# A gated cross-attention and mixture-of-experts block: three-product scores, a staged GpSimd, and new orders of work

## The reference, cut to what matters

```python
# x: (4, 256, 128)   ctx: (4, 256, 96)   2 heads of 64, 32 experts of 64, top 4
def _L0_xattn_ref(x, latents, mask, ...):
    xn = layernorm(x, ln_x_g, ln_x_b);  ln = layernorm(latents, ln_l_g, ln_l_b)
    q = ln @ Wq.T
    kv = jnp.concatenate([xn @ Wkv.T, ln @ Wlkv.T], axis=1)      # 512 keys
    k, v = (kv[..., :INNER], kv[..., INNER:])
    qn = rmsnorm(q, qn_g) * SCALE;  kn = rmsnorm(k, kn_g)
    attn = jnp.einsum('bhid,bhjd->bhij', qn, kn)                 # masked, softmax
    out = jnp.einsum('bhij,bhjd->bhid', attn, v)
    return out @ Wo.T + bo
def _L0_ffn_ref(x, expert_sel, keys, values):
    gates = jax.nn.sigmoid(jnp.einsum('nd,ed->ne', xt, expert_sel))
    sel_val, sel_idx = jax.lax.top_k(gates, 4)                   # gate_full: the 4 kept
    scores = jax.nn.relu(jnp.einsum('nd,edf->nef', xt, keys)) * gate_full[:, :, None]
    return jnp.einsum('nef,efv->nv', scores, values)
x = x + jnp.tanh(g_xattn[0]) * _L0_xattn_ref(ctx_768, _layernorm(x), mask, ...)
x = x + jnp.tanh(g_ffn[0]) * _L0_ffn_ref(_layernorm(x), expert_sel, keys, values)
```

## Time and profile before

| | |
|---|---|
| median of three runs | 115.79 us |
| the profiled execution's own time | 115.75 us |
| its span on the core | 114.0 us |
| TensorE busy | 105.8 us (93%) |
| VectorE busy | 95.0 us (83%) |
| ScalarE busy | 65.6 us (58%) |
| GpSimd busy | 16.0 us (14%) |
| share of TensorE in the chain that ended last | 74% |

### The profile page before, as it was taken

One profiled execution on the slowest core, in us unless ns is written; L12 is line 12 of the kernel. 1 busy time (PEld: TensorE's weight loads), 2 busy tenths in 40 slices (PEclk: granted clock), 3 DMA queues, 4 the chain that ended last, 5 costly groups with the idle time before them and its releaser, 6 DMA issues.

```text
span 114.0 us, 2086 instructions
## 1 busy us (share of the span) xinstructions
PE 105.8 (93%) x644; PEld 86.1 (76%) x644; DVE 95.0 (83%) x309; ACT 65.6 (58%) x148; POOL 16.0 (14%) x26
## 2 busy tenths in 40 slices
...
GB/s 86 223 179 397 376 10 3 3 6 0 0 0 0 6 0 0 0 3 6 0 12 49 297 270 255 178 255 198 3 12 285 299 244 229 214 126 83 0 30 154
DMA packets 7112, 12.78 MB, mean 112 GB/s; under 512 B 894, under 2 KB 2558, under 8 KB 6847
## 3 DMA queue, kind: packets, MB, share of 16 engines
...
HBM read 12.00 MB, written 0.66 MB: 111 GB/s over the span
## 4 chain that ended last, share of the span: by engine, by line
PE 74%; ACT 12%; DMA 4%; DVE 3%; SPq 3%; issue 1%; DVEq 1%
PE bank L724 13%; PE bank L726 13%; PE bank L725 13%; PE bank L862 10%; PE bank L849 5%; DMA bo<-wb_in 4%; PE bank L916 3%; PE bank L754 3%; PE bank L783 3%; PE bank L794 2%; PE bank L820 2%; PE bank L847 2%; ACT cx L594 1%; ACT kT L657 1%; PE bank L887 1%
## 5 line engine op out<-in xcount | busy, mean ns | idle before, releaser
L701 ACT ACTIVATE hid_hi<-keys 128x512 fp32r<-128x512 f32 x28 | 17.4, 632 | 16.8 <-DVE keys L535 13.1
L535 DVE SCALAR_TENSOR_TENSOR keys<-bank,inT 128x512 f32<-128x512 f32 x32 | 21.2, 686 | 1.1 <-PE bank L726 0.8
L552 DVE TENSOR_TENSOR hid_lo<-keys,hid_hi 128x512 fp32r<-128x512 f32 x28 | 18.4, 686 | 0.1
L862 PE MATMUL bank<-vw,prob 128*128 128x129 f32 x128 | 15.7, 278 | 0.2 <-ACT prob L670 0.2
L862 PEld LDWEIGHTS bank<-vw,prob 128*128 128x128 f32 x128 | 14.8, 191 | 1.0 <-issue 1.0
L724 PE MATMUL bank<-xm_hi,k_lo 128*128 128x512 f32 x32 | 13.7, 427 | 0.0
L726 PE MATMUL bank<-xm_hi,k_hi 128*128 128x512 f32 x32 | 12.5, 391 | 0.0
L725 PE MATMUL bank<-xm_lo,k_hi 128*128 128x512 f32 x32 | 12.5, 390 | 0.0
L445 DVE CUSTOM_DVE_ANT_0 junk<-bank,mask_b 128x512 bf16<-128x512 f32 x16 | 10.4, 689 | 2.0 <-PE bank L820 1.8
L724 PE MATMUL bank<-hid_hi,v_lo 128*128 128x512 f32 x28 | 11.3, 402 | 0.0
L670 ACT ACTIVATE prob<-bank 128x512 f32<-128x512 f32 x16 | 8.7, 594 | 4.0 <-PE bank L849 3.8
...
## 6 DMA issues: line engine op xcount, KB each, us to landing
...
```

What stands on the lines that cost most here:

```text
L535: dve.scalar_tensor_tensor(hid[:, n % 3, :], bank[H_BANK[n % len(H_BANK)]][:, :], 0.0, gated[:, n % SLOTS, :], ALU.max, ALU.mult).then_inc ...
L552: dve.tensor_tensor(hid_lo[:, m % RING, :], hid[:, n % 3, :], hid_hi[:, m % RING, :].bitcast(F32), ALU.subtract).then_inc(hid_lo_ready, 1)
L701: act.activation(hid_hi[:, m % RING, :], hid[:, n % 3, :], ACT.Copy).then_inc(hid_hi_ready, 1)
L862: last = pe.matmul(bank_of(b, OUT + t)[:, WOA * a:WOA * a + WOA], prob[:, b % 2, a, j, P * t:P * t + P], vw[:, b, j, a, :], start=(j == 0) ...
```

## The change

- **Scores.** `qT`, `kT` in f32 and `round_qk` go. ScalarE writes the rounded `qT_hi`, `kT_hi` straight from PSUM; a new stage `turn_qk` on VectorE computes `qT_lo`, `kT_lo` = PSUM times gain minus the rounded part. Each f32 product of `weights` becomes three fp32r products. `row_max` reuses the banks, so it now waits for the low parts too.
- **GpSimd** gets a table, POOL_ORDER. It takes over the Newton steps (four operations there, since its step is written without the fused form), `xn` and `xm`, the split of the selection weights, the `+ 1` of the sigmoid and the scaling of `bo`.
- **Residual.** `turn_res` transposes straight into the accumulator banks, ahead of the `down` sums, with no copy; tanh(g_ffn) moves into the gates. `finish` only copies: ScalarE for the first half, VectorE for the second.
- **Orders.** All tables are new. On ScalarE `constants` comes ahead of the first `stats_in` and no longer holds the scaling of `bo`. The 24 `warm` stages stay, 15 instead of 19 of them ahead of the first transposes.

```diff
-    warm 13, warm 14, warm 15, warm 16, warm 17, warm 18, turn_in 0, warm 19, warm 20, project 0, turn_in 1,
-    fold 0, project 1, vctx 0, vlat 0, turn_in 2, vlat 1, warm 21, warm 22, turn_qk 0, vctx 1, warm 23, vlat 2,
+    warm 13, warm 14, turn_in 0, warm 15, warm 16, warm 17, fold 0, project 0, turn_in 1, vlat 0, warm 18,
+    warm 19, project 1, warm 20, vctx 0, vlat 1, turn_in 2, vctx 1, turn_qk 0, warm 21, vctx 2, turn_qk 1,
...
+POOL_ORDER = """
+    norm_in 0, norm_in 1, mask 0, norm_in 2, scale_bo 0, newton_qk 0, newton_qk 1, split_sel 0, add_bias 0,
+    norm_in 3, newton_qk 2, low_keys 0, newton_qk 3, add_bias 1, low_values 0, low_values 1, low_keys 1,
+    norm_mid 0, low_keys 2, low_keys 3, norm_mid 1, add_one 0, add_one 1, norm_mid 2, low_values 2, add_one 2,
+    norm_mid 3, low_values 3, add_one 3
...
+            def newton(y, v, w):
+
+                then(pool.tensor_tensor(w[:, 1, :], y, y, ALU.mult))
+                then(pool.tensor_tensor(w[:, 2, :], w[:, 1, :], v, ALU.mult))
+                then(pool.tensor_scalar(w[:, 1, :], w[:, 2, :], -0.5, 1.5, ALU.mult, ALU.add))
+                return pool.tensor_tensor(w[:, 3, :], w[:, 1, :], y, ALU.mult)
...
+            def norm_in(b):
+                pool.wait_ge(var_ready, b + 1)
+                pool.tensor_scalar(nm_in[:, b, :], mv_in[:, b, BT:, 0], -1.0, None, ALU.mult)
+                pool.wait_ge(y0_in, b + 1)
+                then(newton(rs_in[:, b, 0, :], var_in[:, b, :], rs_in[:, b, :, :]))
+                pool.tensor_tensor(nb_in[:, b, :], nm_in[:, b, :], rs_in[:, b, 3, BT:], ALU.mult).then_inc(nb_ready, 1)
+                for t in range(BT):
+                    j = BT * b + t
+                    pool.tensor_scalar(xn[:, j, :], x[:, j, :], mv_in[:, b, t, 0:1],
+                                       rs_in[:, b, 3, t:t + 1], ALU.subtract, ALU.mult).then_inc(xn_ready, 1)
...
+            def turn_qk(b):
+
+                dve.wait_ge(qk_hi_ready, 2 * b + 1)
+                dve.scalar_tensor_tensor(qT_lo[:, b, :], bank_of(b, TURN_QK + 1)[:, 0:S], gq[:, :],
+                                         qT_hi[:, b, :].bitcast(F32), ALU.mult, ALU.subtract).then_inc(qk_lo_ready, 1)
+                dve.wait_ge(qk_hi_ready, 2 * b + 2)
+                dve.scalar_tensor_tensor(kT_lo[:, b, :], bank_of(b, TURN_QK)[:, :], vec(V_KG),
+                                         kT_hi[:, b, :].bitcast(F32), ALU.mult, ALU.subtract).then_inc(qk_lo_ready, 1)
...
                 for b in range(HB * h, HB * h + HB):
-                    dve.wait_ge(midT_ready, b + 1)
-                    dve.wait_ge(down_done, EC * (h + 1))
-                    dve.scalar_tensor_tensor(res[:, b, :], bank[ACC_BANK[h]][:, S * (b % HB):S * (b % HB) + S],
-                                             tanh_g[:, 1:2], x_midT[:, b, :], ALU.mult, ALU.add).then_inc(res_ready, 1)
-
+                    dve.tensor_copy(res[:, b, :], acc(b)).then_inc(res_ready, 1)
...
-                act.wait_ge(in_bo, 16)
-                act.activation(bo[:, :], bo[:, :], ACT.Copy, scale=tanh_g[:, 0:1]).then_inc(bo_ready, 1)
...
-                    if i >= 2:
+                    if i < 2:
+                        pe.wait_ge(qk_lo_ready, 2 * b + i + 1)
+                    else:
                         pe.wait_ge(max_taken, n - 1)
...
                     for a in range(HEADS):
-                        last = pe.matmul(o[a], kT[rows[a], b, keys_t], qT[rows[a], b, :], start=False, stop=True)
+                        pe.matmul(o[a], kT_lo[rows[a], b, keys_t], qT_hi[rows[a], b, :], start=False, stop=False)
+                    for a in range(HEADS):
+                        pe.matmul(o[a], kT_hi[rows[a], b, keys_t], qT_lo[rows[a], b, :], start=False, stop=False)
+                    for a in range(HEADS):
+                        last = pe.matmul(o[a], kT_hi[rows[a], b, keys_t], qT_hi[rows[a], b, :], start=False, stop=True)
...
-                    last = pe.transpose(res_bank(b)[:, P * t:P * t + P], x_mid[:, BT * b + t, :], ident[:, :])
-                last.then_inc(midT_done, 1)
+                pe.wait_ge(gateT_ready, HB * (b // HB + 1))
+                for t in range(BT):
+                    pe.matmul(acc(b)[:, P * t:P * t + P], x_mid[:, BT * b + t, :], ident[:, :],
+                              start=(b % HB == 0 and t == 0), stop=False, is_transpose=True)
```

More of the change, by code:

```diff
@@ new lines @@
+    warm 19, project 1, warm 20, vctx 0, vlat 1, turn_in 2, vctx 1, turn_qk 0, warm 21, vctx 2, turn_qk 1,
+    warm 22, row_max 0.0, warm 23, vlat 2, turn_in 3, row_max 0.1, project 2, vlat 3, row_max 1.0, turn_max 0,
+    vctx 3, weights 0.0, row_max 1.1, project 3, turn_qk 2, turn_max 1, weights 0.1, weights 1.0, row_max 2.0,
+    attend 0.0, attend 0.1, turn_qk 3, weights 1.1, row_max 2.1, row_max 3.0, attend 1.0, turn_max 2,
+    row_max 3.1, weights 2.0, attend 1.1, turn_mid 0, weights 2.1, turn_max 3, select 0, weights 3.0, attend 2.0,
@@ L72 @@
 """
 DVE_ORDER = """
-    stats_in 0, stats_in 1, norm_in 0, norm_in 1, scale_wo 0, stats_in 2, sum_qk 0, norm_in 2, sum_qk 1,
-    norm_qk 0, stats_in 3, norm_qk 1, norm_in 3, row_max 0.0, row_max 0.1, row_max 1.0, turn_max 0, sum_qk 2,
-    norm_qk 2, sum_qk 3, row_max 1.1, norm_qk 3, turn_max 1, row_max 2.0, row_max 2.1, row_max 3.0, turn_max 2,
-    out_proj 0, stats_mid 0, row_max 3.1, norm_mid 0, out_proj 1, turn_max 3, stats_mid 1, turn_mid 0,
-    norm_mid 1, select 0, turn_mid 1, select 1, out_proj 2, stats_mid 2, norm_mid 2, out_proj 3, turn_mid 2,
@@ L84 @@
[L84 to L85 removed]
+    stats_in 0, scale_gq 0, stats_in 1, scale_wo 0, stats_in 2, sum_qk 0, stats_in 3, sum_qk 1, norm_qk 0,
+    norm_qk 1, turn_qk 0, row_max 0.0, turn_qk 1, row_max 0.1, sum_qk 2, turn_max 0, row_max 1.0, norm_qk 2,
+    row_max 1.1, turn_max 1, turn_qk 2, sum_qk 3, row_max 2.0, norm_qk 3, out_proj 0, turn_qk 3, row_max 2.1,
+    row_max 3.0, turn_max 2, stats_mid 0, row_max 3.1, out_proj 1, turn_mid 0, turn_max 3, stats_mid 1, select 0,
@@ L86 @@
+    up 1.8, up 1.9, split 1.7, split 1.8, split 1.9, up 1.10, up 1.11, up 1.12, split 1.10, split 1.11, up 1.13,
+    split 1.12, up 1.14, up 1.15, split 1.13, split 1.14, split 1.15, finish 1
 """
 ACT_ORDER = """
-    stats_in 0, constants 0, stats_in 1, norm_in 0, turn_in 0, norm_in 1, project 0, turn_in 1, stats_in 2,
-    fold 0, project 1, norm_in 2, sum_qk 0, vctx 0, vlat 0, turn_in 2, sum_qk 1, vlat 1, turn_qk 0, stats_in 3,
-    vctx 1, round_qk 0, turn_qk 1, norm_in 3, round_qk 1, turn_in 3, vlat 2, vctx 2, split_keys 0, project 2,
@@ L91 @@
-    vlat 3, vctx 3, sum_qk 2, weights 0.0, project 3, weights 0.1, sum_qk 3, turn_qk 2, round_qk 2, split_keys 1,
-    split_values 0, turn_qk 3, round_qk 3, weights 1.0, split_keys 2, split_keys 3, weights 1.1, weights 2.0,
-    stats_mid 0, turn_mid 0, split_values 1, weights 2.1, stats_mid 1, weights 3.0, select 0, turn_mid 1,
-    weights 3.1, select 1, turn_gates 0, turn_gates 1, stats_mid 2, turn_mid 2, split_values 2, select 2,
-    stats_mid 3, split 0.4, split 0.5, split 0.6, split 0.7, turn_mid 3, turn_res 0, split 0.8, turn_gates 2,
@@ L96 @@
-    select 3, split 0.9, split 0.10, split_values 3, turn_gates 3, split 0.11, split 0.12, turn_res 1,
-    split 0.13, turn_res 2, split 0.14, split 0.15, split 1.0, split 1.1, split 1.2, split 1.3, turn_res 3,
+    constants 0, stats_in 0, norm_in 0, stats_in 1, turn_in 0, norm_in 1, fold 0, project 0, turn_in 1,
+    stats_in 2, vlat 0, sum_qk 0, project 1, norm_in 2, vctx 0, stats_in 3, sum_qk 1, turn_in 2, turn_qk 0,
+    vctx 1, vlat 1, turn_qk 1, norm_in 3, vctx 2, vlat 2, turn_in 3, project 2, sum_qk 2, split_keys 0, vlat 3,
```

212 lines of the change are left out of this document (103 added, 109 removed).

## The result

The changed kernel takes **118.80 us** (median of 4, 118.03 to 119.64); the kernel before takes 116.07 in runs beside it (115.44 to 116.58). The ratio is 1.024, 95% interval 1.013 to 1.035: slower, though the interval does not settle whether by more than 2%. Forecast were 112.0 and 109.5 to 114.8. The profiled execution took 118.03 with a span of 116.2 (before 114.0).

What follows compares the result with a forecast made beforehand. The prediction took TensorE, and the places where it waits, to bound the kernel. From 115.75 us it summed -1.5 (scores), -2.7 (head), +0.5 (middle) and 0 (rest) to 112.05, say 112.0, range 109.5 to 114.8.

Steps and rivals of the forecast that it cites:

- term 2: Head, up to the first scores: an earlier first transposed input and less ScalarE work bring them forward, -2.7 us.
- term 3: Between first scores and experts: new waits for GpSimd's normalisation nearly cancel against a vanished wait for gates, +0.5 us.
- Bound: Whole kernel: TensorE, 93% busy and 74% of the chain, bounds it, so the question is where it waits.
- Term 1: Scores: three fp32r pairs at 0.115 replace the f32 part of 0.44 in each of 16 key tiles, -1.5 us.
- rival of heads not side by side: Scores: the new products' heads don't run side by side, or each waits for its load; 116.9 us, chance 0.09.
- term 4: The rest, mainly the experts: TensorE's work there covers the changes on other engines, 0 us.
- GpSimd is the new chain: Head and middle: GpSimd's dependent step costs 0.40, the head gives only 1.0, the middle costs 2.0; 115.2 us, chance 0.15.
- the mechanism that I gave for "slower": Scores: heads of the new products not side by side, or each waiting for its load; 116.9 us, chance 0.09.
- The clock: Sign of being wrong on the whole: TensorE's clock, granted in full, falls in one of the head's gaps; no size given.

Runs made afterwards that it cites:

- e6: The changed kernel with the old scores (one float32 product, round_qk back on ScalarE, turn_qk off VectorE): 119.44 us, 1.038 of the kernel before.
- e11: The changed kernel with GpSimd's sixteen xn and xm tile instructions cut to 16 of 128 columns, a price probe: 113.78 us, 0.982 of the kernel before.
- e2: The changed kernel with the sixteen xn and xm tiles back on VectorE, Newton steps still on GpSimd: 119.91 us, 1.030 of the kernel before.
- e3: The kernel before with the scores part of the change alone, normalisation and Newton steps staying on VectorE: 121.87 us, 1.055 of the kernel before.
- e5: The kernel of e2 with only GpSimd's order changed, to keep its long tiles apart from VectorE's tiles: 117.00 us, 1.010 of the kernel before.
- e1: The changed kernel with GpSimd's sixteen xn and xm tiles copied (operands 0.0 and 1.0), not normalised: 115.84 us, 1.004 of the kernel before.

## Why the prediction was wrong

**The step that failed** is in term 2: "`xn` (0.60 on VectorE, taken as 0.6 on GpSimd) ends at 7.0 and is in time". Two tiles take 1.59 there, and term 3 uses the same price. I had bounded GpSimd's small steps from both sides and given the tile VectorE's price without a bound, although had GpSimd at 1.27 for a tile of 512 columns, and although I quoted the warning about elementwise tiles (the Trainium skill, "GPSIMD Engine Reference", 4.1) a few lines on and applied it to the small steps alone. Sixteen tiles are 7.4 us more than on VectorE (16 times 0.46), on the path in the head and at three of the four `turn_mid`, the third of them among the experts.

- **Bound.** Right: TensorE, and what it waits for.
- **Term 1, scores, -1.5.** Period 0.48, so 16 times 0.07 is -1.1; two of the three pairs 0.11 to 0.12 as forecast, and with 0.48 under 0.55 for the tile the rival of heads not side by side is out. The bf16 pair and the first fp32r pair take 0.25 together (29.05 to 29.30) where I had 0.225. By the rule of the Trainium skill ("TensorE: Matmul & The Clock Gate", Part 1) I had estimated 0.50 for the tile, by the rows 0.455; the trace lies between. That the whole part measures -1.4 to -1.5 (e6) is luck for this term: 0.9 of it lies in the head, whose saving on `round_qk` I had booked under term 2.
- **Term 2, head, -2.7.** Up to `cx` right (6.55 for 6.4); a dependent GpSimd step is 0.27 to 0.30, inside 0.22 to 0.40. Then `inT` 8.84 for 7.7, `row_max` 21.78 for 19.3, first scores 29.05 for 26.5: -0.14. With narrow tiles (e11) `inT` is at 8.19, `row_max` at 20.38 and the first scores at 26.93: -2.3. So the tile is most of the miss; what is left (`row_max` 1.1 late, made up in part behind it) may be the 0.43 for 0.30 and was not taken apart.
- **Term 3, middle, +0.5.** From the first scores to the end of the span 84.8 before, 87.15 now: +2.3, and +3.4 beside the scores' -1.1. The statistics and roots took about the time that I had worked out, two tiles 1.59 where I had 0.6, and the wait comes at batches 0, 1 and 2. With narrow tiles the same stretch is 85.0, still +1.3 beside the scores' -1.1 where I had +0.5 with term 4.
- **Term 4, experts, 0.** Wrong in size: `turn_mid 2` inside the experts waits for tiles too (TensorE idle 0.95 of 49.96: 0.62 for the tiles, 0.33 for `xm_lo` behind them).
- **The rival "GpSimd is the new chain"** (the first in the list, which the text ahead of it calls the second) named the engine but the wrong price: a step of 0.40, and 115.2. No rival had a tile price, and the mechanism that I gave for "slower" was another.
- **The clock** was named as a sign of being wrong on the whole, but without a price or a chance. At full clock the miss is 6.0 us, by the median 6.8. In e2, e3 and e5 the fall follows idle stretches of TensorE; that it did so in the changed kernel is not shown, since its trace is at full clock throughout.

With the price of e11, 0.43, the changed kernel is at 113.7, 1.7 above the sum of 112.05. For the 0.30 that I had taken I estimate 112.5 to 113, from e11 and the slope between e1 and e11 (0.6 of what GpSimd saves, 16 times 0.13). About 0.4 of the rest is term 1. The cause of what then remains stays open.
